# A fused convolution, attention and wavelet block on one core: another order of the first image's stage and of the last tail, with buffers of the tail in the probabilities' place

## The chip, the cores and the metric

The kernel runs on one core of one Trainium2 chip. The metric is the device time of one execution in microseconds (us). The program names the engines so: PE is TensorE (matrix products), DVE is VectorE, ACT is ScalarE, POOL is GpSimd, SP is SyncE, which here only issues DMAs.

## What is computed

The input x has 8 images of 256 channels and 32x32 positions, all float32. Three steps, with L = 1024 positions as tokens:

```python
# 1: attention over positions, 8 heads of 32 channels, on group-normed channels
qkv = einsum('oc,bcl->bol', w_qkv, group_norm(x)) + b_qkv
weight = softmax(einsum('bct,bcs->bts', q * scale, k * scale), axis=1)
x = x + w_proj @ einsum('bts,bcs->bct', weight, v) + b_proj
# 2: linear attention on layer-normed tokens t, with rotated queries and keys
q, k = elu(ln(t) @ Wqk + bqk) + 1
z = 1 / (q . mean(k) + 1e-6);  kv = rope(k)^T v / n
t = t + rope(q) kv * z + lepe(v)          # v = ln(t); lepe: 3-tap depthwise conv
# 3: feed-forward on the low band of a Haar transform of ln(t)
t = t + ffn(ln(t))                        # pair sums, interpolation, fc1, gelu, fc2, back
```

## The kernel before

**The stages.** The work of an image is cut in two. The first half is the softmax attention: 64 units, one for each pair of a key block (8), a head (4) and a head group (2). The second half, "post", is everything behind it: projection, layer norm, linear attention, feed-forward. The program is software-pipelined over images in *bodies*: body i runs the 64 units of image i, the post work of image i-1, and prepares queries, keys and values of image i+1. A prologue comes before body 0, the epilogue ("tail") holds the post work of image 7. So body 0 ("first") has no post work, bodies 1 to 6 are "steady", body 7 is "last".

**A unit.** PE makes the scores of one head and key block into one of two PSUM buffers (`scores`, L653, 128x1024), DVE takes the negated maximum (`maximum`, L1053), ACT takes the exponential with its sum (L914) into `probs`. PE's scores of unit s+1 wait for the exponential of unit s-1, whose buffer they take. After four units DVE inverts the sums (`invert_sums`, L1059), POOL scales the values (`scale_values`, L1330), and PE weighs them (`weigh_values`, L668).

**The order.** Each engine has one queue in which everything else is put between units. Tables of numbers (`PE_FIRST`, `DVE_FIRST`, `PE_TAIL` and so on) give for each piece of work the unit behind which it stands in its engine's queue; `due` reads them. In the tail, where there are no units, the numbers (0 to 63) are only an order. Inside one number the order is that of the table's keys. SP's queue is given by `SP_ORDER`.

**Names.** `pq`, `pk`, `pv` with group 0 or 1: tiles of the next queries, keys, values (L680, L692), each split by ACT (L955) and DVE (L1098) into two parts that SP stacks. `w1`: a weight folded once, in the first body (PE L840, DVE copy L1262). `stats`, `moments`, `gn`, `squares`, `affine`, `apply`: group norm of the next image. `load`: its load. `warm`: two matmuls on constants, whose result nobody reads (`keep_warm`, L867); in the tail they wait only for the last attention copy. In the tail: `proj` (L727), `x1T` (L707), `lnT` (L715), `qk` (L741, eight tiles: group, query or key, half), `kT` (L749, keys to tokens), `kv` (L757), `den`, `denT`, `out` (L781), `uT` (L707), `ll` (L795), `fc1` (L800), `fc2` (L805), `rT` (L715), `rows` (L812).

**Buffers of the tail.** `elu` (L1236) writes queries into `q_ch` (two groups) and keys into `k_ch`, which has room for one group: keys of group 1 wait for the `kT` that reads those of group 0. DVE turns keys (L1181, L1183) into `rot_tok`, with room for one group: turns of group 1 wait for `kv` of group 0. `turn_q` (L507 to L514) multiplies a half-exchanged copy `q_half` of the queries by sines, the queries in place by cosines (after `den` has read them), and adds the two. In the tail POOL turns group 0, and DVE the cosine product and sum of group 1 (`late_turn`). `lepe` taps of channels 0 to 127 are DVE's in the tail (`lepe_tail`, L1250), the others POOL's (L1386, L1389). `probs` holds 2 x 4 x 1024 columns and is not used in the tail.

```python
elif n in (2, 4):
    eng.wait_ge(q_turned[g], 2 * HG * DMA * (b + 1))
    eng.wait_ge(made["den"], b + 1)
    eng.tensor_tensor(q_ch[:, g, :], q_ch[:, g, :], const("cos_ch"), ALU.mult).then_inc(turn_step[g], 1)
```

## Time and profile before

| | |
|---|---|
| median of 3 runs (lowest, highest) | 1364.28 us (1364.17, 1369.44) |
| the profiled execution | 1364.11 us |
| its span, first to last instruction | 1362.3 us |
| mean granted TensorE clock | 0.976 |
| busy share of the span | PE 91%, DVE 73%, ACT 65%, POOL 34% |
| first maximum, first body to second, last maximum | 28.84, 168.00, 1264.60 us |

The first maximum of a body marks its begin here. A busy share is an average over stages; the rows further down are read by stage. "Clock" is the share of 2.4 GHz that TensorE was granted in a stretch: it has two levels, 1.00 (2.4 GHz) and 0.50 (1.2 GHz), and a value between is a mean of the two.

### The profile page before, as it was taken

The numbers are of one execution on the slowest core, as the hardware profiler recorded it, in microseconds if no ns is written. First come the engines' busy times: TensorE is split into PE (matmuls) and PEld (weight loads), VectorE is DVE, ScalarE is ACT, GpSimd is POOL, SyncE is SP. The second block draws the span as 40 slices with busy tenths as digits, with TensorE's granted clock in tenths as the row PEclk, the third lists the DMA queues.
The fourth block names the chain that finished last, engine by engine and source line by source line (L and its number), as shares of the span: only waits on it lengthen the run. The fifth ranks groups of instructions, "written<-read, shape, count | busy, mean of one in ns | idle before, by whom it ended". The sixth has DMA issues, their size and how long they took to land.

```text
span 1362.3 us, 22187 instructions
## 1 busy us (share of the span) xinstructions
PE 1235.3 (91%) x7972; PEld 644.5 (47%) x7972; DVE 995.1 (73%) x1609; ACT 879.5 (65%) x1457; POOL 467.4 (34%) x621
## 2 busy tenths in 40 slices
PE   6888899899998999899998999989998999979796
PEld 5544444544445454445444444454544444444373
DVE  3666687857889487866888578884879678884663
ACT  1666667675776668676775767766685767757422
POOL 2001017520285015630185203840166301850351
PEclk9998999999999999999999999999999999999897
DMA  8242415123442236223351234422262234300210
GB/s 275 58 108 45 106 40 134 34 63 101 110 112 47 52 109 139 48 63 93 92 116 27 66 117 101 105 57 58 88 140 48 62 93 110 80 15 0 80 33 31
DMA packets 51180, 110.84 MB, mean 81 GB/s; under 512 B 15456, under 2 KB 15840, under 8 KB 50816
## 3 DMA queue, kind: packets, MB, share of 16 engines
q1 hardware_dynamic: 48400, 100.39, 30.3%
q0 software_dynamic: 2480, 8.78, 2.3%
q8 instruction: 64, 1.05, 0.3%
q14 instruction: 44, 0.36, 0.1%
q10 hardware_dynamic: 192, 0.26, 0.1%
HBM read 21.81 MB, written 8.39 MB: 22 GB/s over the span
## 4 chain that ended last, share of the span: by engine, by line
PE 54%; DVE 29%; ACT 7%; issue 4%; POOL 2%; DMA 2%; SPq 1%; DVEq 0%; ACTq 0%; POOLq 0%
DVE negmax L1053 15%; PE ps_s L653 13%; PE ps_o L668 7%; PE work L741 6%; ACT probs L914 5%; PE work L680 4%; PE work L800 4%; PE work L727 4%; PE work L692 3%; DVE tok L1129 3%; DVE ln_st L1118 3%; PE work L805 3%; PE work L781 2%; DVE lo L1098 1%; PE work L715 1%
## 5 line engine op out<-in xcount | busy, mean ns | idle before, releaser
L914 ACT ACTIVATE probs<-ps_s,negmax 128x1024 f32<-128x1024 f32 x512 | 571.0, 1115 | 328.0 <-DVE negmax L1053 323.3
L1053 DVE TENSOR_REDUCE negmax<-ps_s 128x1 f32<-128x1024 f32 x512 | 618.8, 1216 | 220.0 <-PE ps_s L653 218.2
L653 PE MATMUL ps_s<-q_st,k_st 128*128 128x512 f32 x1024 | 407.8, 482 | 54.7 <-ACT probs L914 42.7
L653 PEld LDWEIGHTS ps_s<-q_st,k_st 128*128 128x128 f32 x1024 | 165.1, 192 | 294.4 <-ACT probs L914 163.3
L1330 POOL TENSOR_TENSOR v_scaled<-v_tok,rsums 128x128 f32<-128x128 f32 x128 | 56.0, 438 | 580.3 <-DVE rsums L1059 580.3
L668 PE MATMUL ps_o<-probs,v_scaled 128*32 128x512 f32 x2048 | 249.9, 606 | 1.3 <-POOL v_scaled L1330 1.3
L680 PE MATMUL work<-xg,w_qkv 128*128 128x512 f32 x256 | 120.7, 597 | 2.7 <-ACT xg L927 2.7
L741 PE MATMUL work<-ln_ch,w_qk 128*128 128x512 f32 x240 | 115.0, 601 | 3.6 <-DVE k_ch L1236 3.6
L668 PEld LDWEIGHTS ps_o<-probs,v_scaled 128*32 128x32 f32 x2048 | 53.9, 110 | 129.9 <-issue 117.7
L1389 POOL TENSOR_TENSOR x<-x,csum 128x1024 f32<-128x1024 f32 x45 | 107.5, 2389 | 2.5
L914 ACT ACTIVATION_READ_ACCUMULATOR probs<-ps_s,negmax 128x1 f32 x512 | 99.6, 195 | 0.0
L1361 POOL TENSOR_TENSOR ln_var<-ln_mv,con 128x2 f32<-128x2 f32 x64 | 12.9, 202 | 184.4 <-DVE ln_mv L1123 184.4
L800 PE MATMUL work<-band,w 128*128 128x512 f32 x120 | 63.6, 666 | 7.8 <-ACT band L996 6.0
L680 PEld LDWEIGHTS work<-xg,w_qkv 128*128 128x128 f32 x256 | 46.6, 189 | 44.2 <-issue 38.3
L692 PEld LDWEIGHTS work<-w_qkv,xg 128*128 128x128 f32 x512 | 63.6, 196 | 4.1 <-DVE lo L1098 1.4
L692 PE MATMUL work<-w_qkv,xg 128*128 128x128 f32 x512 | 64.0, 280 | 0.0
L741 PEld LDWEIGHTS work<-ln_ch,w_qk 128*128 128x128 f32 x240 | 43.0, 188 | 42.7 <-issue 29.8
L727 PE MATMUL work<-att,w_proj 128*128 128x512 f32 x120 | 56.8, 597 | 0.0
L1386 POOL TENSOR_SCALAR csum<-ln_ch,par 128x1024 f32<-128x1024 f32 x45 | 54.9, 1221 | 0.0
L805 PE MATMUL work<-shared,w 128*128 128x512 f32 x112 | 52.6, 592 | 0.0
L999 ACT ACTIVATE shared<-work,par 128x512 f32<-128x512 f32 x60 | 41.0, 689 | 16.2 <-PE work L800 16.1
L988 ACT ACTIVATE t<-work,par_elu 128x512 f32<-128x512 f32 x60 | 41.2, 687 | 10.9 <-PE work L741 10.9
(157 smaller groups left out, 1448.5 us busy)
## 6 DMA issues: line engine op xcount, KB each, us to landing
q_st<-hi SPq DMA_DIRECT2D x128, 128.0 KB, 2.4
q_st<-lo SPq DMA_DIRECT2D x120, 128.0 KB, 2.4
k_st<-t SPq DMA_DIRECT2D x224, 64.0 KB, 2.0
k_st<-hi SPq DMA_DIRECT2D x128, 64.0 KB, 2.8
k_st<-lo SPq DMA_DIRECT2D x128, 64.0 KB, 3.2
x<-in_x SPq DMA_DIRECT2D x8, 1024.0 KB, 6.1
out_x<-ln_ch SPq DMA_DIRECT2D x16, 512.0 KB, 2.8
xg<-in_x POOLq DMA_DIRECT2D x7, 1024.0 KB, 8.6
```

The costliest lines, as they stand in the source:

```text
L653: mm = pe.matmul(ps_s[s % 2][:, half * HALF:half * HALF + HALF], k_st[:, h, j * P:j * P + P], q_st[g][:, h, half * HALF:half * HALF + HALF ...
L668: mm = pe.matmul(ps_o[D * h:D * h + D, cols], v_scaled[:, j % 2, D * h:D * h + D], probs[:, j % 2, h, cols], start=(j == 0), stop=(j == NB ...
L680: mm = pe.matmul(bank(tile)[:, :], w_qkv[:, c, col:col + P], xg[:, c, half * HALF:half * HALF + HALF], start=(c == 0), stop=(c == NC - 1))
L692: mm = pe.matmul(bank(tile)[:, P * n:P * n + P], xg[:, c, P * nb:P * nb + P], w_qkv[:, c, col:col + P], start=(c == 0), stop=(c == NC - 1))
L727: mm = pe.matmul(ps[:, :], w_proj[:, g, P * c:P * c + P], att[:, g, half * HALF:half * HALF + HALF], start=(g == 0), stop=(g == 1))
L741: mm = pe.matmul(ps[:, :], w_qk[:, c, col:col + P], ln_ch[:, c, 1 + half * HALF:1 + half * HALF + HALF], start=(c == 0), stop=(c == NC - 1))
L800: pe.matmul(ps[:, :], w1[:, P * n:P * n + P], band[:, :], start=True, stop=True)\
L805: mm = pe.matmul(ps[:, :], w2[:, k, :], hid[:, k, :], start=(k == 0), stop=(k == 7))
L914: act.activation(probs[:, j % 2, h, :], ps_s[s % 2][:, :], ACT.Exp, bias=negmax[:, s % 4:s % 4 + 1], accum_out=sums[:, j % 2, h:h + 1]).th ...
L1053: dve.tensor_reduce(negmax[:, s % 4:s % 4 + 1], ps_s[s % 2][:, :], AX_X, ALU.max, negate=True)\
L1330: pool.tensor_tensor(v_scaled[:, j % 2, :].rearrange("p (h d) -> p h d", h=HG), v_tok[g][:, j, :].rearrange("p (h d) -> p h d", h=HG), r.t ...
L1389: pool.tensor_tensor(x1[:, c, :], x1[:, c, :], lepe_product, ALU.add).then_inc(lepe_step, 1)
```

## The change

It has three parts.

1. **The first body** has other numbers on PE, ACT, DVE and POOL. The work in it is the same.
2. **The tail** has other numbers on the four engines, and the eight `qk` tiles come in another order: all queries first (both groups), then all keys. It was queries, keys of group 0, then queries, keys of group 1. It has 41 warm pairs instead of 28.
3. **Places in the tail.** Turned queries of both groups, keys of group 1 and turned keys of group 1 are written into `probs` (`q_home`, `k_home`, `turns_home`). With that three waits are left out there: the cosine product's on `den`, group 1's keys' on `kT`, and group 1's turns' on `kv`.

`keep_warm` also leaves out the later `fc2` steps when it looks for the tile whose bank it writes. SP's order is unchanged, and so is the order in bodies 1 to 7.

```diff
 PE_FIRST = {
-    "w1": (25, 28), "pq1": (12, 12), "pv1": (2, 5), "pk1": (19, 22),
...
-    "pq0": (44, 44), "pk0": (47, 52), "pv0": (44, 56),
+    "w1": (25, 27), "pq1": (11, 12), "pv1": (0, 0), "pk1": (19, 20), "gn": (39,), "pq0": (43, 44),
+    "pk0": (49, 56), "pv0": (45, 56), "values": (6, 10, 14, 18, 22, 26, 30, 34, 38, 42, 46, 50, 54, 58, 62),
...
-QK_ORDER_TAIL = [(g, is_k, half) for g in range(NG) for is_k in (0, 1) for half in range(2)]
+QK_ORDER_TAIL = [(g, is_k, half) for is_k in range(2) for g in range(NG) for half in range(2)]
...
+        def q_home(b, g):
+            return q_ch[:, g, :] if b + 1 < B else probs[:, 1, g, :]
+
+        def k_home(b, g, half):
+            return k_ch[:, half, :] if g == 0 or b + 1 < B else probs[:, 1, 2 + half, 0:HALF]
+
+        def turns_home(b, g):
+            if g == 0 or b + 1 < B:
+                return rot_tok
+            return probs[:, 0, 0:2, :].rearrange("p r (b c) -> p r b c", b=NB)
...
             elif n in (2, 4):
                 eng.wait_ge(q_turned[g], 2 * HG * DMA * (b + 1))
-                eng.wait_ge(made["den"], b + 1)
-                eng.tensor_tensor(q_ch[:, g, :], q_ch[:, g, :], const("cos_ch"), ALU.mult).then_inc(turn_step[g], 1)
+                if b + 1 < B:
+                    eng.wait_ge(made["den"], b + 1)
+                eng.tensor_tensor(q_home(b, g), q_ch[:, g, :], const("cos_ch"), ALU.mult).then_inc(turn_step[g], 1)
             else:
                 eng.wait_ge(turn_step[g], 2 * (b + 1))
-                eng.tensor_tensor(q_ch[:, g, :], q_ch[:, g, :], q_half[g], ALU.add).then_inc(qrot_done[g], 1)
+                eng.tensor_tensor(q_home(b, g), q_home(b, g), q_half[g], ALU.add).then_inc(qrot_done[g], 1)
...
                 elif name == "kT":
                     g, half = n // 2, n % 2
-                    if g == 1:
+                    if g == 1 and b + 1 < B:
 
                         dve.wait_ge(made["kv"], 2 * b + 1)
...
                 g, is_k, half = qk_order(b)[m]
-                if is_k and g == 1:
+                if is_k and g == 1 and b + 1 < B:
 
                     dve.wait_ge(made["kT"], 4 * b + half + 1)
```

**PE, first body, units 43 to 47.** L653/L666 are scores, L668/L681 weighed values, L680/L693 two matmuls for each query or key tile, L692/L705 a value tile, L867/L883 warm pairs (the numbers before and after the slash are the lines before and after the change). Before:

```order
L653 MATMUL ps_s<-q_st,k_st 128x512 x4
L680 MATMUL work<-xg,w_qkv 128x512 x4
L692 MATMUL work<-w_qkv,xg 128x128 x8
L653 MATMUL ps_s<-q_st,k_st 128x512 x4
L668 MATMUL ps_o<-probs,v_scaled 32x512 x8
```

After:

```order
L666 MATMUL ps_s<-q_st,k_st 128x512 x2
L693 MATMUL work<-xg,w_qkv 128x512 x2
L666 MATMUL ps_s<-q_st,k_st 128x512 x2
L693 MATMUL work<-xg,w_qkv 128x512 x2
L666 MATMUL ps_s<-q_st,k_st 128x512 x2
L705 MATMUL work<-w_qkv,xg 128x128 x8
L666 MATMUL ps_s<-q_st,k_st 128x512 x2
L681 MATMUL ps_o<-probs,v_scaled 32x512 x8
```

Two query tiles and a value tile stood together between scores; now each has scores ahead of it and behind it.

**PE, tail, from the sixth to the eighth query/key tile.** L741/L754 are two matmuls for each `qk` tile, L749/L762 the keys' transposes, L867/L883 warm matmuls. Before (the sixth tile ends the first row):

```order
L741 MATMUL ps_s<-ln_ch,w_qk 128x512 x8
L741 MATMUL work<-ln_ch,w_qk 128x512 x2
L867 MATMUL ps_o<-con 128x128 x20
L741 MATMUL work<-ln_ch,w_qk 128x512 x2
L749 MATMUL ps_s<-con,k_ch 128x128 x16
```

After:

```order
L754 MATMUL ps_s<-ln_ch,w_qk 128x512 x8
L754 MATMUL work<-ln_ch,w_qk 128x512 x2
L762 MATMUL work<-con,k_ch 128x128 x4
L754 MATMUL ps_s<-ln_ch,w_qk 128x512 x2
L762 MATMUL ps_s<-con,k_ch 128x128 x4
L883 MATMUL ps_o<-con 128x128 x6
L762 MATMUL ps_s<-con,probs 128x128 x4
```

The ten warm pairs ahead of the eighth tile are gone, and a transpose of group 0's keys stands there.

**DVE, tail, from the taps to the key turns.** L1250/L1267 are the taps, L1236/L1253 the elus, L1181/L1198 and L1183/L1200 one turn together. Before:

```order
L1250 SCALAR_TENSOR_TENSOR x<-ln_ch,par,x 128x1024 x3
L1236 SCALAR_TENSOR_TENSOR shared<-work,par_elu,t 128x512 x2
L1236 SCALAR_TENSOR_TENSOR k_ch,ksum<-ps_s,par_elu,t 128x512 x2
L1236 SCALAR_TENSOR_TENSOR shared<-ps_s,par_elu,t 128x512 x2
L1236 SCALAR_TENSOR_TENSOR k_ch,ksum<-work,par_elu,t 128x512 x2
L1181 TENSOR_TENSOR shared<-ps_s,con 128x512
```

After:

```order
L1253 SCALAR_TENSOR_TENSOR shared<-work,par_elu,t 128x512 x2
L1267 SCALAR_TENSOR_TENSOR x<-ln_ch,par,x 128x1024 x2
L1253 SCALAR_TENSOR_TENSOR shared<-ps_s,par_elu,t 128x512 x2
L1253 SCALAR_TENSOR_TENSOR k_ch,ksum<-ps_s,par_elu,t 128x512 x2
L1253 SCALAR_TENSOR_TENSOR probs,ksum<-work,par_elu,t 128x512
L1267 SCALAR_TENSOR_TENSOR x<-ln_ch,par,x 128x1024
L1253 SCALAR_TENSOR_TENSOR probs,ksum<-ps_s,par_elu,t 128x512
L1198 TENSOR_TENSOR shared<-work,con 128x512
```

The taps moved behind the second and the seventh elu, and keys of group 1 go to `probs`.

## Rows read from the trace of the kernel before

**Rows 1.** The page: granted clock by slice, two groups of instructions.
```profile
PEclk9998999999999999999999999999999999999897
...
L1389 POOL TENSOR_TENSOR x<-x,csum 128x1024 f32<-128x1024 f32 x45 | 107.5, 2389 | 2.5
...
L988 ACT ACTIVATE t<-work,par_elu 128x512 f32<-128x512 f32 x60 | 41.2, 687 | 10.9 <-PE work L741 10.9
```

**Rows 2.** Busy time by stretch: first body, two steady ones, the tail.
```profile
core 0: us, PE busy (x) PEld busy (x) DVE busy (x) ACT busy (x) POOL busy (x), PEclk, DMA share, GB/s
28.84:168.00 139.16, 115.12 (x614) 65.31 (x614) 89.41 (x102) 83.94 (x140) 9.06 (x25) 0.94 0.35 84
...
640.29:798.97 158.68, 147.44 (x958) 73.91 (x958) 121.69 (x199) 109.71 (x183) 59.78 (x77) 0.99 0.35 84
...
957.20:1113.01 155.81, 146.16 (x958) 73.41 (x958) 121.89 (x199) 109.56 (x183) 59.75 (x77) 1.00 0.35 85
...
1264.60:1362.30 97.70, 77.61 (x624) 50.24 (x624) 53.66 (x114) 29.24 (x46) 33.68 (x37) 0.90 0.18 50
```

**Rows 3.** Busy time by stretch: pieces of the first body.
```profile
28.84:48.98 20.14, 15.29 (x90) 11.96 (x91) 10.28 (x10) 9.56 (x16) 0.40 (x1) 0.83 0.41 94
48.98:98.34 49.36, 41.82 (x218) 21.11 (x217) 34.24 (x39) 30.52 (x51) 3.18 (x7) 1.00 0.37 89
98.34:114.69 16.35, 12.05 (x74) 6.65 (x72) 11.81 (x17) 9.53 (x18) 1.92 (x8) 1.00 0.24 56
114.69:134.57 19.88, 17.64 (x82) 9.78 (x83) 11.87 (x14) 13.81 (x21) 1.96 (x6) 0.83 0.15 33
134.57:150.97 16.40, 14.23 (x76) 6.97 (x74) 10.31 (x11) 9.26 (x17) 0.80 (x2) 1.00 0.60 153
150.97:168.00 17.03, 14.08 (x80) 8.83 (x80) 10.90 (x14) 11.26 (x19) 0.80 (x2) 0.90 0.30 72
```

**Rows 4.** Order of time, DVE, first body: start, us, instruction, [idle before <-releaser].
```profile
87.22 0.69 DVE L1262 COPY w<-work 128x512 f32<-128x512 f32 x1 [2.63 <-PE work L840]
...
113.48 0.16 DVE L1082 COPY gn_grp<-work 128x4 f32<-128x4 f32 x1 [2.06 <-PE work L698]
```

**Rows 5.** Order of time, PE, first body (a float32 matmul has two records).
```profile
116.13 1.22 PE L653 MATMUL ps_s<-q_st,k_st 128*128 128x512 f32 x2 [2.68 <-ACT probs L914]
...
125.03 3.67 PE L680 MATMUL work<-xg,w_qkv 128*128 128x512 f32 x8 [0.36 <-ACT xg L927]
128.61 2.05 PE L692 MATMUL work<-w_qkv,xg 128*128 128x128 f32 x16
```

**Rows 6.** Order of time, PE, tail.
```profile
1299.53 4.63 PE L867 MATMUL ps_o<-con 128*128 128x128 f32 x40
...
1330.48 1.91 PE L715 MATMUL work<-con,t 128*128 128x128 f32 x8 [2.58 <-DVE t L520]
1335.54 3.65 PE L795 MATMUL ps_s<-con,csum 128*128 128x64 f32 x16 [3.15 <-POOL csum L1395]
```

**Rows 7.** Order of time, DVE and POOL, tail, up to the first normalised product.
```profile
1289.37 5.95 DVE L1250 SCALAR_TENSOR_TENSOR x<-ln_ch,par,x 128x1024 f32<-128x1024 f32 x3 [3.37 <-ACT x L933]
...
1289.72 3.20 POOL L1389 TENSOR_TENSOR x<-x,csum 128x1024 f32<-128x1024 f32 x1
...
1306.35 0.75 DVE L1236 SCALAR_TENSOR_TENSOR k_ch<-work,par_elu,t 128x512 f32<-128x512 f32 x1 [4.47 <-PE ps_s L749]
...
1307.43 0.75 DVE L1236 SCALAR_TENSOR_TENSOR k_ch<-work,par_elu,t 128x512 f32<-128x512 f32 x1 [0.32 <-ACT t L991]
...
1313.28 0.69 DVE L1181 TENSOR_TENSOR shared<-ps_s,con 128x512 f32<-128x512 f32 x1 [2.57 <-PE work L757]
...
1316.01 2.71 DVE L511 TENSOR_TENSOR shared<-shared,con 128x1024 f32<-128x1024 f32 x1
...
1321.19 0.69 DVE L1199 TENSOR_TENSOR t<-ps_s,zden 128x512 f32<-128x512 f32 x1 [0.34 <-PE ps_s L781]
```

**Rows 8.** Order of time, tail: the band's copy on ACT and its last step.
```profile
1339.28 0.59 ACT L996 COPY band<-ps_s 128x512 f32<-128x512 f32 x1 [6.27 <-PE ps_s L795]
...
1354.67 0.75 DVE L1212 SCALAR_TENSOR_TENSOR band<-ps_s,par,band 128x512 f32<-128x512 f32 x1 [16.46 <-PE ps_s L805]
```

More of the change, by code:

```diff
@@ L129 @@
 PE_TAIL = {
[L130 to L134 removed]
+    "rT": (41, 41, 46, 46), "out": (31, 31, 34, 34), "proj": (0, 0, 1, 3), "uT": (29, 32, 35, 39),
@@ L135 @@
+    "x1T": (3, 3, 9, 9), "qk": (13, 13, 15, 15, 15, 16, 16, 17), "kT": (16, 17, 18, 19), "ll": (43,),
+    "warm": (3, 3, 3, 7, 9, 9, 9, 9, 12, 12, 12, 13, 17, 17, 17, 18, 23, 24, 29, 30, 31, 31, 34, 35, 35, 35, 35, 36, 37, 37, 37, 37, 38, 39, 39, 39, 39, 41, 41, 41, 54, 54),
+    "fc1": (46, 46, 46, 46, 46, 47, 47, 53), "den": (21,), "rows": (54, 57), "fc2": (48, 49, 53, 53),
+    "kv": (26, 28), "denT": (24,), "lnT": (9, 9, 12, 12),
 }
 ACT_TAIL = {
-    "x1T": (0, 0, 0, 2), "den": (35,), "bias": (17,), "lnT": (4, 7, 7, 10), "ll": (40,),
@@ L145 @@
 }
 POOL_TAIL = {
-    "pairs": (50, 54, 56, 57), "rsqrt1": (0, 0, 0, 0), "kmean": (21,), "lepe": (2, 3, 4, 7, 13, 31),
-    "rsqrt2": (40, 46, 46, 48), "turn": (11, 34, 34, 39),
+    "rsqrt2": (37, 39, 51, 53), "rsqrt1": (3, 3, 4, 10), "turn": (21, 30, 30, 35), "pairs": (46, 51, 53, 55),
+    "lepe": (13, 16, 17, 18, 19, 23), "kmean": (25,),
 }
@@ L852, in keep_warm @@
                 order = [t for s in range(UNITS) for t in due("PE", kind, s)]
-                later = [t for t in order[order.index(("warm", n)):] if t[0] not in ("values", "warm")]
+                later = [t for t in order[order.index(("warm", n)):]
+                         if t[0] not in ("values", "warm") and t not in LATER_STEPS]
                 tile = later[0] if later else LISTS[i + 2][0]
@@ L1178, in angle @@
                             .rearrange("p (n o d) -> p n o d", n=4, o=1)[:, :, :, a:z].to_broadcast([P, 4, HG, z - a])
-                    straight, turned = (rot_tok[:, r, rows, :].rearrange("p n (h d) -> p n h d", h=HG) for r in range(2))
+                    straight, turned = (turns_home(b, g)[:, r, rows, :].rearrange("p n (h d) -> p n h d", h=HG)
+                                        for r in range(2))
                     dve.tensor_tensor(straight, k_t, angle("cos_tok", 0, D), ALU.mult)
@@ L1235, in elu @@
                 at = 2 * g + half
-                dve.scalar_tensor_tensor(out=k_ch[:, half, :] if is_k else q_ch[:, g, half * HALF:half * HALF + HALF],
+                dve.scalar_tensor_tensor(out=k_home(b, g, half) if is_k else q_ch[:, g, half * HALF:half * HALF + HALF],
                                          in0=bank(("qk", m))[:, :],
```

39 lines of the change are left out of this document (18 added, 21 removed).

## The prediction

> **What bounds the kernel now.** I read the page first, then the busy time by body, then by pieces of the first body, then the order of time on TensorE (PE), VectorE (DVE), ScalarE (ACT) and GpSimd (POOL) in the two places that the change touches. The page gives no single full engine: PE's granted clock is 9 or 8 tenths in nearly every slice, so PE runs at 2.4 GHz with short falls to 1.2 GHz [rows 1]. By body, the first one takes 139.16 us, the other seven 151.6 to 158.7, and the tail after the last maximum 97.70 [rows 2]. In the first body PE is busy 115.12 of 139.16 us, in the fastest steady body 146.16 of 155.81: the steady bodies are full of PE work, the first body and the tail are full of waits. The loop there is a ring: scores on PE, maximum on DVE, exponential on ACT, and back to PE for the next scores in the same bank. Whatever stands in one of the three queues ahead of its next unit stretches the ring.
>
> The program moves nothing in the six steady bodies or the last; SP's order is word for word the same. So the sum has two terms.
>
> **How I worked them out.** I laid the new order beside the old one, engine by engine, kept for each instruction the duration of its row, and started each when the one ahead on its engine was through and what it waits for was done. Laid out in this way, the old first body comes to 138.7 us where the trace has 139.16, and the old tail to within 0.5 us; that is how far I trust the layout.
>
> **Term 1, the first body, piece by piece** [rows 3]. Same instructions, other places.
> - Units 0 to 7: 20.14 now, 20.4 new. Both second-group value tiles now stand behind the scores of unit 1, in the half-clock stretch (0.83 in this piece), and delay unit 2; by unit 3 the two orders are level, since the old one has the first of them one unit later anyway.
> - Units 8 to 31: 49.36 now, 48.1 new. The two query tiles of group 1 run together between scores, as those of group 0 do for 3.67 us [rows 5]; they now stand on either side of a pair of scores. DVE's copy of the folded weights idles 2.63 us for a PE tile issued just before [rows 4], with the next maximum behind it; it now stands two maxima later. That idle time is mostly PE work that stays, so I count 1.3 for both and not their sum.
> - Units 32 to 39: 16.35 now, 14.3 new. Moments and group copy are in one place on DVE; the copy idles 2.06 us [rows 4] while PE's next scores wait 2.68 us [rows 5]. New: the moments one maximum earlier than the copy's pair, so POOL's two small products and PE's means run below the maxima. 2.1 saved.
> - Units 40 to 47: 19.88 now, 17.0 new. Two query tiles (3.67) and a value tile (2.05) stand together between scores, 5.7 us [rows 5]; now they stand behind three different units. Part of the loss is the fall of the clock to 0.83 here, which follows the 2.68 us wait that goes.
> - Units 48 to 55: 16.40 now, 15.1 new. Reciprocals come straight behind the fourth exponential at every step, where the old order had them one unit late, so PE meets its value step ready.
> - Units 56 to 63: 17.03 now, 16.3 new. A key tile and a value tile now share a place, about 3.7 us together, which costs some 0.8; against that the clock is 0.90 in the old piece, and I expect one fall less.
>
> The new pieces sum to 131.2 us against 139.16: **8.0 less**. Bounds: with no half-clock stretch at all the same layout gives 126.8 (12.4 less); with one more such stretch where PE is densest, 134 (5 less). If only the clock-free waits on DVE went (2.63 and 2.06) it would be 4.7 less. I take 8.0 because the waits named are all on the ring.
>
> **Term 2, the tail** (times from the span's start, tail begins at 1264.60).
> - To the first projected tiles nothing changes: residual and band rows land as before. One of the two late rows of the previous image now stands behind the first statistics; the second store goes out some 3 us later, and lands well before its reader, the copies of the normalised channels.
> - *Up to the last key.* PE now has ten warm pairs in 40 matmuls, 4.63 us, ahead of the eighth query/key tile [rows 6], and DVE idles 4.47 us at the seventh because the keys' place must first be read [rows 7]. Both go: one warm pair is left among these tiles, and second keys are put in the probabilities' place. In exchange DVE's three long taps are split two and one among the elus. By the layout the first two taps hold the third and fourth elus until 1298.4 and 1299.0; the keys follow by ACT's pace (a step has a mean of 687 ns [rows 1] and a tile has two, so some 1.3), and the last, behind a tap, starts at 1305.3; it is 1307.43 now [rows 7]: 2.1 gained.
> - *Key turns.* The second pair of turns idles 2.57 us on the first key-value product [rows 7], since it needs its place. That wait goes. Its two turns and a small product took from 1313.28 to 1316.01, so a turn takes some 1.25; four in a row end at 1311.0, where they end at 1315.8 now. 4.8 gained in all.
> - *Turned queries.* DVE's cosine product took 2.71 us [rows 7] with POOL's sum beside it. The new place has the same neighbour, and comes a little earlier in it: 3.05. The wait on the denominators' product goes too, but it was met long before, so it is worth nothing. The first normalised product starts at 1316.4 and not at 1321.19 [rows 7]: still 4.8.
> - *Second norm to the band.* From there to ACT's copy of the band is 18.1 us now (1321.19 to 1339.28), 17.1 new: PE's 16 pair matmuls took 3.65 us at half clock after waits of 2.58 and 3.15 [rows 6]; POOL's pair sums are now spread, and 18 warm pairs stand on PE around this stretch where 6 do now. 1.0 more.
> - *Feed-forward.* 15.4 us from that copy to the band's last step (1354.67) [rows 8]; 14.6 new, since the first tiles do not meet a half clock. 0.8 more. The end is unchanged.
>
> 4.8 + 1.0 + 0.8 = 6.6; I take off 0.4 for a half-clock stretch that I expect at the first norm as now: **6.2 less**. Bounds: 3.1 less if the half clock comes back for ten microseconds in the second norm; 12.7 less if DVE and POOL never held each other up.
>
> The last bound fails by a row: three DVE taps took 5.95 us and POOL's sum beside them 3.20 [rows 7], where 45 such sums have a mean of 2389 ns [rows 1]. They take turns, whole instructions at a time, and my sum keeps that. The Trainium skill says so too (SBUF — State Buffer, "Who interferes with whom": a VectorE instruction with two SBUF inputs and a GpSimd one that reads SBUF hold a shared port against each other for the whole instruction), and that rule speaks against this change, which sets DVE's taps and turned queries beside POOL's sums again. Without it the tail would gain the 12.7.
>
> **Sum.** 8.0 + 6.2 = 14.2 off the profiled execution's 1364.11 us (span 1362.3 plus 1.8 around it) gives 1349.9; its median over the runs, 1364.28, stands 0.2 above it. I say **1350.0 us**, 1.0% faster. About 0.5%, or 6.8 us, is what a measurement of this kernel can tell from no change.
>
> **Rivals.**
> 1. *The clock takes part of it back* (0.13). A further half-clock stretch in the first body (+2.8) and the one in the second norm (+3.1): 1356. For it: the old pieces show such stretches at three places of the first body [rows 3]; the six steady bodies, one program, differ by 2.9 us (155.81 to 158.68), the longer one at a clock of 0.99 and the shorter at 1.00 [rows 2]. Against it: fewer waits over 2 us remain on PE.
> 2. *The first body doesn't follow its waits* (0.06): what is moved is PE work, its sum stays, and another unit is stretched in place of each. Then only the tail gains: 1364.1 - 6.2 = 1357.9, within 0.5%. Against it: PE stands idle 24 us there.
> 3. *The change does not do what it says in the tail* (0.04): the keys' place is free, but DVE finds POOL's sums in the way at each tap and turn, and the tail ends as now. With the first body's gain: 1356.
> 4. *Slower* (0.03): the clock is not given back after the first half-clock stretch, since two value tiles now stand in it and the ring starts later. Pieces with a clock of 0.83 took 20.14 and 19.88 where 16.35 and 16.40 are usual, some 3.6 us a piece; from four pieces on nothing is gained, and with six pieces, 22 us, it is 1372. Against it: the clock came back within the first piece with less work offered.
>
> **Chances.** Forecast 0.74, rivals 0.13, 0.06, 0.04, 0.03. The range takes the forecast's own bounds, 1345.6 (no half clock in the first body) to rival 1 with one microsecond over it: 1345 to 1357. Faster by over 0.5% holds forecast, rivals 1 and 3: 0.91. Within 0.5%: 0.06. Slower: 0.03.
>
> **What would show it.** The first body from first to last maximum about 131 us, no DVE wait over 1.5 us at the copies of weights and group means, and no more than one tile between pairs of scores but at two places. In the tail: no DVE idle time over 1 us between the elus and the last key turn, first normalised product about 51.8 us after the last maximum (56.6 now), the 16 pair matmuls under 3 us. Wrong, if the first body is above 135 or the tail above 95 us; then the clock row of that stretch says whether it was rival 1, and if that is full, the ring has another bound than I think.

## The result and the profile after

Over four runs the changed kernel has a median of **1350.66 us** (1347.21 to 1352.56), the kernel before 1364.91 (1364.17 to 1369.44). The ratio is 0.9885, 95% interval 0.9859 to 0.9911: 1.2% faster, 1350.0 was forecast. The profiled execution took 1351.87 us with a span of 1350.1; before it was 1362.3, so 12.2 us went from the span. The forecast of 14.2 us less fits the medians (14.25 less) better than it fits the stages: the closeness of 1350.66 to 1350.0 is in part luck. The stretch between the two stages has the same program in every kernel here and takes 1091.6 to 1097.2 us in thirteen profiles.

Busy time by stretch of the changed kernel (first body; its six pieces by units 0 to 7, 8 to 31, 32 to 39, 40 to 47, 48 to 55, 56 to 63; the tail), with the columns of [rows 2] and [rows 3]:

```profile
29.19:161.16 131.97, 111.43 (x615) 63.84 (x616) 89.89 (x102) 84.35 (x140) 8.98 (x25) 0.97 0.36 87
1257.65:1350.10 92.45, 80.25 (x680) 53.87 (x680) 54.02 (x113) 28.66 (x46) 33.45 (x37) 0.96 0.19 53
29.19:50.08 20.89, 15.48 (x90) 12.24 (x91) 10.93 (x11) 9.54 (x16) 0.39 (x1) 0.84 0.38 90
50.08:97.67 47.59, 42.02 (x218) 21.56 (x217) 33.95 (x38) 31.18 (x52) 3.17 (x7) 1.00 0.37 92
97.67:112.18 14.51, 11.82 (x74) 6.73 (x72) 11.75 (x17) 10.48 (x19) 1.19 (x4) 1.00 0.27 64
112.18:129.45 17.27, 15.17 (x83) 8.19 (x83) 11.93 (x15) 12.95 (x21) 2.63 (x9) 1.00 0.14 31
129.45:144.55 15.10, 12.51 (x72) 6.50 (x70) 10.37 (x12) 10.19 (x17) 0.80 (x2) 1.00 0.67 175
144.55:161.16 16.61, 14.43 (x85) 8.61 (x86) 10.96 (x13) 10.01 (x17) 0.80 (x2) 1.00 0.29 71
```

The first body lost 7.19 us, the tail 5.25. From the second body's first maximum to the last maximum it is 1096.49 us, where it was 1096.60: nothing moved there. The first maximum comes 0.35 later. 7.19 + 5.25 + 0.11 - 0.35 = 12.2. PE's busy time fell by 3.7 us in the first body with the same instructions: that is matmuls which no longer run at half clock. In the tail it rose by 2.6 with 14 warm pairs more (the table has 42 of them, not 41, and the row counts differ by 56, four records a pair). The counts in PE's rows are records, two for each float32 matmul: a row of x8 is two warm pairs, and a key-value product of 64 matmuls has 128 records, which the prediction and the expectations call matmuls.

The tail of the changed kernel in order of time; first DVE, then GpSimd, PE, ACT and DVE again:

```profile
1283.71 0.75 DVE L1253 SCALAR_TENSOR_TENSOR shared<-work,par_elu,t 128x512 f32<-128x512 f32 x1 [4.35 <-ACT t L1007]
1286.57 4.67 DVE L1267 SCALAR_TENSOR_TENSOR x<-ln_ch,par,x 128x1024 f32<-128x1024 f32 x2 [0.39 <-ACT x L949]
1298.28 0.74 DVE L1253 SCALAR_TENSOR_TENSOR probs<-ps_s,par_elu,t 128x512 f32<-128x512 f32 x1
1303.33 0.74 DVE L1200 TENSOR_TENSOR probs<-ps_s,con 128x256 f32<-128x256 f32 x2
1304.19 3.02 DVE L524 TENSOR_TENSOR probs<-shared,con 128x1024 f32<-128x1024 f32 x1
1307.56 0.29 DVE L1179 TENSOR_TENSOR kv_c<-ps_s,con 128x128 f32<-128x128 f32 x1 [0.34 <-PE ps_s L771]
1311.27 0.69 DVE L1216 TENSOR_TENSOR t<-ps_s,zden 128x512 f32<-128x512 f32 x1 [1.57 <-PE ps_s L796]
...
1294.92 2.36 POOL L1406 TENSOR_TENSOR x<-x,csum 128x1024 f32<-128x1024 f32 x1
1299.17 0.19 POOL L1418 TENSOR_TENSOR ksum_g<-ksum 128x2 f32<-128x2 f32 x1 [1.90 <-DVE probs L1253]
1303.78 2.35 POOL L527 TENSOR_TENSOR probs<-probs,t 128x1024 f32<-128x1024 f32 x1
...
1304.22 0.87 PE L771 MATMUL ps_s<-tok,probs 128*32 128x32 f32 x78 [0.46 <-DVE probs L1200]
1306.64 0.88 PE L771 MATMUL ps_s<-tok,probs 128*32 128x32 f32 x50 [1.55 <-issue]
1308.36 1.91 PE L883 MATMUL ps_o<-con 128*128 128x128 f32 x8
1310.06 1.10 PE L796 MATMUL ps_s<-kv_c,probs 128*128 128x128 f32 x8
...
1327.69 0.59 ACT L1012 COPY band<-ps_s 128x512 f32<-128x512 f32 x1 [3.88 <-PE ps_s L810]
1342.44 0.75 DVE L1229 SCALAR_TENSOR_TENSOR band<-work,par,band 128x512 f32<-128x512 f32 x1 [15.00 <-PE work L820]
```

Counted from the last maximum (1257.65 here, 1264.60 before): last key elu 40.63 (42.83 before), key turns through at 46.4 (51.2), first normalised product 53.62 (56.59), the band's copy on ACT 70.04 (74.68), the band's last step 84.79 (90.07). These milestones measure the experiments too: six steady bodies of about 157 us and single half-clock stretches move a whole run by some 3 us either way. A stage has less of this, but not nothing. The first body takes 131.12 to 132.66 us in six profiles with the changed order and 138.65 to 141.78 in four with the old one; the changed tail takes 90.80, 91.47, 92.45 and 92.54 us in four profiles with the same instructions. A difference of one profile that is smaller than that is not read as an effect below.

### The profile page after: what moved, and what is told of

Its sections match the earlier page's. It is cut to its first block, busy times and chain, and to the rows that moved or that the text cites. A ratio compares the mean times of both kernels' runs of the same rounds, so it can differ in the third digit from the quotient of the medians.

```text
span 1350.1 us, 22293 instructions
## 1 busy us (share of the span) xinstructions
PE 1234.0 (91%) x8028; PEld 646.0 (48%) x8028; DVE 996.0 (74%) x1609; ACT 878.0 (65%) x1457; POOL 466.6 (35%) x621
## 3 DMA queue, kind: packets, MB, share of 16 engines
q8 instruction: 65, 1.06, 0.3%
## 4 chain that ended last, share of the span: by engine, by line
PE 52%; DVE 29%; ACT 8%; issue 5%; POOL 3%; SPq 2%; DMA 1%; DVEq 0%; POOLq 0%; ACTq 0%
DVE negmax L1069 15%; PE ps_s L666 12%; PE ps_o L681 7%; PE work L754 6%; ACT probs L930 5%; PE work L693 5%; PE work L815 4%; PE work L740 4%; PE work L820 3%; PE work L705 3%; DVE tok L1145 3%; DVE ln_st L1134 3%; PE work L796 1%; DVE lo L1114 1%; PE work L728 1%
## 5 line engine op out<-in xcount | busy, mean ns | idle before, releaser
L666 PE MATMUL ps_s<-q_st,k_st 128*128 128x512 f32 x1024 | 407.3, 481 | 51.3 <-ACT probs L930 39.0
L666 PEld LDWEIGHTS ps_s<-q_st,k_st 128*128 128x128 f32 x1024 | 163.8, 191 | 294.0 <-ACT probs L930 161.2
L681 PE MATMUL ps_o<-probs,v_scaled 128*32 128x512 f32 x2048 | 250.0, 606 | 1.3 <-POOL v_scaled L1347 1.3
L693 PE MATMUL work<-xg,w_qkv 128*128 128x512 f32 x256 | 121.0, 597 | 2.9 <-ACT xg L943 2.8
L754 PE MATMUL work<-ln_ch,w_qk 128*128 128x512 f32 x236 | 113.1, 601 | 3.4 <-DVE k_ch L1253 3.4
L681 PEld LDWEIGHTS ps_o<-probs,v_scaled 128*32 128x32 f32 x2048 | 53.8, 110 | 128.6 <-issue 116.6
L693 PEld LDWEIGHTS work<-xg,w_qkv 128*128 128x128 f32 x256 | 46.7, 189 | 43.8 <-issue 37.6
L705 PEld LDWEIGHTS work<-w_qkv,xg 128*128 128x128 f32 x512 | 63.6, 196 | 3.7 <-DVE lo L1114 0.7
L705 PE MATMUL work<-w_qkv,xg 128*128 128x128 f32 x512 | 63.8, 280 | 0.0
L754 PEld LDWEIGHTS work<-ln_ch,w_qk 128*128 128x128 f32 x236 | 42.3, 188 | 42.0 <-issue 29.3
L820 PE MATMUL work<-shared,w 128*128 128x512 f32 x128 | 59.8, 592 | 0.0
L1381 POOL TENSOR_TENSOR ln_rs<-ln_var,con 128x2 f32<-128x2 f32 x64 | 44.7, 699 | 5.0
```

What stands on the lines that cost most here:

```text
L666: mm = pe.matmul(ps_s[s % 2][:, half * HALF:half * HALF + HALF], k_st[:, h, j * P:j * P + P], q_st[g][:, h, half * HALF:half * HALF + HALF ...
L681: mm = pe.matmul(ps_o[D * h:D * h + D, cols], v_scaled[:, j % 2, D * h:D * h + D], probs[:, j % 2, h, cols], start=(j == 0), stop=(j == NB ...
L693: mm = pe.matmul(bank(tile)[:, :], w_qkv[:, c, col:col + P], xg[:, c, half * HALF:half * HALF + HALF], start=(c == 0), stop=(c == NC - 1))
L705: mm = pe.matmul(bank(tile)[:, P * n:P * n + P], xg[:, c, P * nb:P * nb + P], w_qkv[:, c, col:col + P], start=(c == 0), stop=(c == NC - 1))
L754: mm = pe.matmul(ps[:, :], w_qk[:, c, col:col + P], ln_ch[:, c, 1 + half * HALF:1 + half * HALF + HALF], start=(c == 0), stop=(c == NC - 1))
L820: mm = pe.matmul(ps[:, :], w2[:, k, :], hid[:, k, :], start=(k == 0), stop=(k == 7))
```

## The experiments

**The two parts by themselves.** One kernel takes the four `_FIRST` tables alone, the other everything but these.

> The kernel before with the changed tables of the first body alone. Theory (two separate gains): the first body takes 131 to 133 us from its first to its last maximum as in the changed kernel (131.96), the tail stays at 97.0 to 98.5 (97.70), the time is 7 us below the kernel before, ratio 0.995. Rival (the shorter first body is bought with places in the tail, or gives something back later): the tail or a body between moves by over 1 us.

> The changed kernel with the first body's old tables: the tail change alone. Theory: tail 92 to 93.5 us (92.45), first body 138 to 140, time 5 to 6 us below the kernel before, ratio 0.996. Rival (the tail's 5.25 us hang on the clock that the shorter first body leaves): tail above 94.5.

The first took 1355.19 us, ratio 0.9928 (0.9903 to 0.9954), below the 0.995 expected. It has no profile of a fast execution, so what its expectation says of first body and tail stays untested. The second took 1357.65, ratio 0.9948 (0.9924 to 0.9972), with a first body of 141.78 us and a tail of 90.80, both outside what was expected (138 to 140, 92 to 93.5). Together the ratios make 0.9876, and the whole change is at 0.9885. The times fit two separate parts of 0.7% and 0.5%. The tail came out 1.65 us *better* than in the changed kernel, with the same instructions. DVE and GpSimd there:

```profile
1312.65 1.21 DVE L525 TENSOR_TENSOR probs<-shared,con 128x1024 f32<-128x1024 f32 x1
...
1312.75 3.32 POOL L528 TENSOR_TENSOR probs<-probs,t 128x1024 f32<-128x1024 f32 x1
```

GpSimd waited 0.46 us more for a transfer there, so its sum was started 0.10 behind DVE's cosine product and not 0.41 ahead of it. DVE took 1.21 us and GpSimd 3.32; in the changed kernel it is 3.02 and 2.35. So one number of the prediction, 3.05 for that product, was the outcome of a race. It is not where the 1.65 us come from: behind the product DVE waits for the second key-value product either way, 1.83 us here and 0.34 in the changed kernel, and its copy of that starts at 49.57 and 49.91 from the last maximum. The rest is the clock: it is full here, and at half for 3.4 us from 49.1 in the changed kernel.

**The places, taken back and by themselves.** The first kernel is the changed one with `q_home`, `k_home` and `turns_home` returning the old places and the waits back:

```diff
-            return q_ch[:, g, :] if b + 1 < B else probs[:, 1, g, :]
+            return q_ch[:, g, :]
...
-                    if g == 1 and b + 1 < B:
+                    if g == 1:
```

> The changed kernel, its orders untouched, but queries, keys and turns of the tail go back to their old places, with the three waits that belong to them. Theory A, the one of the prediction (the waits on the places carry the gain up to the first normalised product): the key turns of group 1 wait some 2.3 us for the first key-value product, and the tail is 2 to 2.5 us longer than the changed kernel's 92.45. Theory B (GpSimd and the port carry it, the places little): DVE starts its turns 1.8 to 2.3 later, but its cosine product then finds GpSimd's sum nearly through and takes 1.3 to 1.6 where it took 3.0; the tail is 0 to 0.8 longer.

The second is the kernel before with the places and without the waits:

> The kernel before with the places in the probabilities' place and the three waits dropped, all orders as before. Theory A (the places carry it): the 4.47 and 2.57 us of DVE's idle time go and the first normalised product starts 2.5 us or more earlier than 56.6 us after the last maximum; tail 95 or less. Theory B (GpSimd's queue carries it): the turns start 1.5 us earlier, DVE's cosine product then stands beside GpSimd's cosine product and takes 2.5 to 3.1 where it began late before, GpSimd's sums end when they did, and the tail is within 0.7 of 97.70.

Old places in the new order: 1349.98 us, ratio 0.989 (0.9861 to 0.992), a tail of 92.98 against 92.45, a difference inside what the changed tail varies by. DVE's third turn waits 2.25 us for the first key-value product, and then its cosine product takes 1.26, since GpSimd's sum is nearly through:

```profile
1301.27 0.69 DVE L1195 TENSOR_TENSOR shared<-ps_s,con 128x512 f32<-128x512 f32 x1 [2.25 <-PE ps_s L768]
...
1304.00 1.26 DVE L521 TENSOR_TENSOR shared<-shared,con 128x1024 f32<-128x1024 f32 x1
```

New places in the old order: 1362.37, ratio 0.9984 (0.9964 to 1.0004), no difference that can be told. Its tail, 100.19, is outside what either theory named. It is longer than 97.70 in part ahead of the places: in its first norm the clock is 0.66 over ten microseconds (0.83 before), and the first elu starts at 31.95 from the last maximum and not at 30.64. From that elu to the first normalised product it is 25.68 us, and 25.95 before: the places give 0.27. Behind that it loses another 1.45 us, where nothing was changed.

```profile
1303.38 0.75 DVE L1254 SCALAR_TENSOR_TENSOR probs<-work,par_elu,t 128x512 f32<-128x512 f32 x1 [4.87 <-ACT t L1008]
...
1309.30 2.92 DVE L525 TENSOR_TENSOR probs<-shared,con 128x1024 f32<-128x1024 f32 x1
1312.26 3.28 DVE L528 TENSOR_TENSOR probs<-probs,att 128x1024 f32<-128x1024 f32 x1
```

The idle time of 4.47 us at the seventh elu went, and 4.87 us came one elu later: the eighth tile is still behind the ten warm pairs. The 2.57 at the third turn went too, and what it gained DVE lost in the cosine product and the sum, each beside one of GpSimd. Theory B named the cosine product nearly right on both sides, 1.26 and 2.92 us. But that GpSimd's queue carries this stretch is not what the traces show. The chain of work that ended last in the kernel before leaves DVE behind its second turn and stays on PE up to the first output tile:

```profile
1310.05 0.67 DVE shared L1183 x2
1310.72 0.14 issue
1310.86 1.10 PE work L757 x69
1311.96 0.88 issue
1312.84 0.39 PE work L757 x21
1313.23 3.77 PE ps_o L867 x32
1317.00 0.44 PE ps_s L774 x4
1317.43 1.23 PE ps_s L757 x82
1318.66 1.09 PE ps_o L867 x8
```

Eight warm pairs (3.77 us) stand there between the two key-value products. The wait of 2.57 us, the cosine product and GpSimd's sums are all beside this chain: GpSimd's last sum ended at 1317.64, 2.4 us before PE came to the tile that needs it. With the places alone PE still makes its first output tile at 1314.88 to 1315.94, just ahead of DVE's first normalised product at 1316.32, so without the port DVE could have gained 0.4 us at most. With the old places in the new order the second key-value product starts 2.5 us later, but without the stall of 1.55 us described below, and ends 1.1 us later. What the eight warm pairs ahead of the second product cost was not run by itself.

**Places and warm pairs.** The kernel with the places alone, and nine pairs fewer:

```diff
@@ PE_TAIL, the warm pairs up to 16
-    "warm": (14, 15, 16, 16, 16, 16, 16, 16, 16, 16, 16, 16)
+    "warm": (14, 15, 16)
```

> The kernel with the places alone, and nine of the ten warm pairs ahead of the eighth query/key tile gone as well; orders otherwise as before. Theory (a place pays only together with the tile that fills it, and GpSimd's queue has the rest): the eighth tile is made 4 us earlier, the last key elu starts 2.5 to 3 us earlier against the first tap than in the kernel with the places alone (12.7 us behind the first elu there, about 9.5 here), but GpSimd reaches the keys' mean only after its sine product and is some 0.8 to 1 us earlier, so the first normalised product gains 1 to 2.5 us against that kernel's 25.7 us behind the first elu. Rival (the places and the pairs are worth their waits, 4.5 and 2.6 us): it gains 4 us or more.

1363.57 us, ratio 0.9971 (0.9948 to 0.9995). The last key elu starts 9.44 us behind the first (12.74 with the places alone, 12.19 before), the first normalised product 24.04 behind it (25.68, 25.95): 1.64 gained, within what the theory gave. The two edits that the prediction priced at 4.47 and 2.57 us of idle time are worth 1.9 together without the rest of the new order. DVE then waits 2.68 us for PE's output tile at the first normalised product. PE had waited 1.33 us for GpSimd's keys' mean, and then made the eight warm pairs, partly interrupted, in 4.2 us (1311.46 to 1315.63). So GpSimd's queue holds PE up to the keys' mean here, and the warm pairs do behind it. In this kernel, as before, GpSimd's last tap sum stands behind the keys' mean:

```profile
1308.58 0.19 POOL L1419 TENSOR_TENSOR ksum_g<-ksum 128x2 f32<-128x2 f32 x1
1308.86 0.35 POOL L1422 TENSOR_TENSOR kmean<-con,ksum_g 128x4 f32<-128x4 f32 x2
1309.16 2.40 POOL L1407 TENSOR_TENSOR x<-x,csum 128x1024 f32<-128x1024 f32 x1
```

In the changed kernel that sum runs at 1294.92, in time in which GpSimd waited for the last key elu. It takes 2.4 us out of the way of the turned queries; GpSimd's turned queries were not what PE waited for in the kernel before.

**The first body's pieces.** The changed kernel, with moments, group copy and the group norm's copy and apply where they were before, and both query tiles and the value tile together again:

```diff
@@ PE_FIRST
-    "pq0": (43, 44), "pk0": (49, 56), "pv0": (45, 56)
+    "pq0": (44, 44), "pk0": (49, 56), "pv0": (44, 56)
@@ DVE_FIRST
-    "stats": (28, 33, 34, 37), "moments": (38,), "gn": (40,)
+    "stats": (31, 32, 37, 38), "moments": (38,), "gn": (38,)
@@ ACT_FIRST
-    "copy": (35, 36), "apply": (41, 42)
+    "copy": (36, 37), "apply": (40, 43)
```

> The changed kernel, but in the first body the moments, group copy and group-norm copy and apply stand where they did before, and so do the next query tiles (both behind one unit, with the first value tile). Theory (each wait is paid on the ring where it stands, as the prediction has it): units 32 to 39 take 16.2 to 16.5 us where they took 14.51, units 40 to 47 18.4 to 20.0 where they took 17.27, the other pieces are unchanged. Rival (the order elsewhere carries it): these pieces move by less than half of that, or others move too.

```profile
97.26:113.67 16.41, 11.64 (x74) 6.66 (x72) 11.79 (x17) 9.28 (x16) 1.18 (x4) 1.00 0.24 56
113.67:135.20 21.53, 18.04 (x82) 9.88 (x83) 11.87 (x15) 13.79 (x21) 2.63 (x9) 0.84 0.14 31
```

Units 32 to 39 took 16.41 (14.51), units 40 to 47 21.53 (17.27) with the clock at 0.84, and every other piece behind unit 8 stayed within 0.02. The first is as the theory has it. The second is above its range (18.4 to 20.0) and above the 19.88 of the kernel before, so the pieces don't simply add. The clock is no sure companion of the tiles that stand together: with the old first body units 40 to 47 took 19.88 us at a clock of 0.83, 19.36 and 19.26 at 0.91 (`places_alone`, `places_and_warm`) and 18.89 at 1.00 (`tail_alone`). Against 17.27 the order is worth about 1.6 us there and the clock up to 1.0.

**The value tiles in the half-clock stretch.**

```diff
@@ PE_FIRST
-    "pv1": (0, 0)
+    "pv1": (5, 8)
@@ DVE_FIRST
-    "pv1": (1, 3)
+    "pv1": (6, 10)
```

> The changed kernel; in the first body the two second-group value tiles stand behind the scores of units 6 and 9 and not both behind those of unit 1. Theory A (in the half-clock stretch they cost twice, and the ring stands still for it): units 0 to 7 take 17.5 to 19.5 us where they took 20.89, units 8 to 15 15.1 to 16.1 where they took 15.09, the first body is 1 to 2.5 us shorter. Theory B (with less work on PE the clock stays low for longer, or the ring pays for the tiles wherever they stand): the first 16 units take 36 us as before.

1344.69 us, ratio 0.9847 (0.981 to 0.9885). Units 0 to 7 took 18.04 us (20.89), units 8 to 15 15.09 (15.09), the first body 129.09. In the changed kernel the two tiles hold PE for 5.42 us in the half-clock stretch, with the scores of unit 2 behind them; behind units 6 and 9 they run at full clock and the ring has room for them. By the stage this gains 2.87 us over the changed kernel, and units 0 to 7 take 20.05 to 21.59 us in the seven profiles with both tiles behind unit 1, 18.04 and 17.91 in the two with them moved. The half clock itself lasted longer here, to 8.7 us behind the first maximum and not to 7.8, and the stage is shorter all the same.

**The second norm's warm pairs.** The changed kernel without 13 of them.

> The changed kernel without 13 of the warm pairs that stand in the second norm of the tail (20 of the 24 matmul rows behind the output tiles, and those ahead of the last transposes). The kernel before had 10.2 us of half clock there, the changed one none. Theory A (the warm pairs keep the clock): a half-clock stretch of 3 to 10 us comes back 55 to 75 us after the last maximum, and from the first normalised product to the band's last step it takes 1 to 3 us more than 31.17 (53.62 to 84.79). Theory B (the shorter waits of the new order keep it): no half clock there, and 31.0 to 31.4 us.

```profile
1306.81:1339.40 32.59, 28.14 (x127) 19.36 (x127) 14.99 (x40) 9.49 (x14) 6.56 (x12) 0.90 0.00 1
```

From first normalised product to the band's last step it took 32.59 us where the changed kernel took 31.17 at a clock of 1.00; before it was 33.48 at 0.85. Theory A: of the 2.31 us gained here, 1.42 are these warm pairs'. This stretch repeats well: 31.15 to 31.17 us at a clock of 1.00 in eight profiles with all the warm pairs. The run took 1351.11 us, which can't be told from 1350.66.

**GpSimd's neighbour.** Two kernels ask why DVE's cosine product takes 3.02 us. One moves GpSimd's cosine product ahead of the keys' mean (`"turn": (21, 30, 30, 35)` becomes `(21, 30, 24, 35)`), one makes GpSimd's last sum for one column only, so it leaves out the rest of that sum and is read for its time alone (one run, 1350.22 us).

> The changed kernel; in the tail GpSimd's cosine product of group 0's queries stands ahead of the keys' mean and of group 1's sine product, in 2 us where GpSimd waited. Theory A (GpSimd and DVE take turns at the port for whole instructions): GpSimd's last sum starts 1.3 to 2 us earlier, DVE's cosine product meets its end at most and takes 1.2 to 1.6 us (3.02 in the changed kernel), the first normalised product starts at 52.3 or earlier; tail 90.5 to 91.5. Theory B (the 3.02 us are no matter of the neighbour): the product still takes 2.5 to 3.1.

> The changed kernel, where in the tail GpSimd's last sum of the turned queries of group 0 is made for one column of 1024 alone; the other columns keep the product without the sum. Theory A (the port): DVE's cosine product takes 1.2 to 1.3 us and ends 1.8 us earlier, DVE then waits for the second key-value product instead, and the first normalised product starts 0.3 to 1.4 us earlier than 53.62. Theory B: it takes 2.5 us or more with no neighbour too.

It took 1.22 us in the one and 1.21 in the other, so the 3.02 us are the neighbour's doing. That does not make it a gain: with the sum cut short DVE waited 1.55 us for the second key-value product (0.34 in the changed kernel). The tail is 90.61 there, within 0.2 us of the changed order's best, and the clock did not fall at 49 us. With the product moved the tail is 93.56 (90.5 to 91.5 was expected), in a run of 1349.85 (median 1347.06, ratio 0.9867, 0.9835 to 0.99). The keys' mean came late, PE waited 1.15 us for it at the denominators, the first key-value product with it, and the second followed at once and stalled for 2.29 us. The expectation named a gain and had not asked who waits for what is moved behind.

**PE's stall.** In the rows above PE stops for 1.55 us behind record 78 of 128 in the second key-value product and waits for nothing that its row shows.

```diff
@@ PE_TAIL, of the warm pairs those of 23 and 24
-    "warm": (23, 24), "kv": (26, 28), "denT": (24,)
+    "warm": (27, 27), "kv": (22, 28), "denT": (27,)
```

> The changed kernel; on PE, in the tail, the first key-value product stands ahead of four warm matmuls and the denominators' transposes and not behind them, so that the two key-value products of 128 matmuls each no longer run within one after the other. The stall: in two profiles PE stops for 1.5 us behind matmul 78 of the second product, with nothing that it waits for. Theory A (instructions are brought in slower than these short matmuls use them up): with 1.5 us more between the products the stall shrinks to under 0.7 us, the clock does not fall at 49 us after the last maximum, and the first normalised product starts within 52.3. Theory B (the stall belongs to something else, such as the results' bank or the probabilities' place): it stays at 1.5 us before the same matmul, and the tail as it is.

```profile
1295.91 0.97 PE L771 MATMUL work<-tok,shared 128*32 128x32 f32 x91 [0.69 <-DVE shared L1200]
1297.03 0.53 PE L771 MATMUL work<-tok,shared 128*32 128x32 f32 x37 [0.15 <-issue]
...
1299.02 0.88 PE L771 MATMUL ps_s<-tok,probs 128*32 128x32 f32 x78
1300.92 0.64 PE L771 MATMUL ps_s<-tok,probs 128*32 128x32 f32 x50 [1.02 <-issue]
```

1346.33 us, ratio 0.986 (0.9831 to 0.9889), tail 91.24. The clock did not fall at 49 us, and the first normalised product starts at 52.43 (52.3 was asked), though the cosine product took 3.04 again. That is no gain that can be told: with the unchanged order of this stretch and a full clock it starts at 51.80 to 52.83 in four profiles. The stall shrank to 1.02 us, where the theory asked for under 0.7, and a short one came in the first product. It follows neither bank nor place, since both products have it now and the first is in another bank.

**All that helped.** Value tiles later, GpSimd's product early, the key-value products apart, DVE's sum of turned queries ahead of its second copy (`"late_turn": (23, 23)`), and no warm matmul between the second key-value product and the first output tile.

> The changed kernel with four edits that the earlier runs point to: value tiles behind the scores of units 6 and 9; GpSimd's cosine product ahead of the keys' mean; the first key-value product ahead of warm matmuls and denominators' transposes, with the warm matmuls between the second one and the first output tile moved behind the output tiles; DVE's sum of the turned queries ahead of its copy of the second key-value product. Theory: first body 128.5 to 129.5 us (131.96), DVE's cosine product under 1.6 us, the stall in the second key-value product about 1 us and off the path, first normalised product 50.3 to 51.5 us after the last maximum (53.62), tail 88.5 to 90.5 (92.45); the time 4 to 6 us below the changed kernel's 1350.66, so 0.985 of the kernel before. Rival (PE waits longer with the warm matmuls gone, and the clock falls in the second norm instead): a half-clock stretch between 50 and 75 us after the last maximum, tail 91 or more.

**1343.24 us** over six runs (1342.14 to 1347.21), ratio 0.9847 (0.9811 to 0.9884); first body 128.99, tail 90.34, first normalised product 51.03, second norm to the band's last step 31.64 at a clock of 1.00.

```profile
1250.76:1341.10 90.34, 79.33 (x680) 52.68 (x680) 53.38 (x113) 28.46 (x46) 34.42 (x37) 0.97 0.19 54
28.56:157.55 128.99, 110.12 (x615) 62.78 (x616) 90.06 (x102) 84.50 (x140) 8.98 (x25) 0.98 0.37 90
```

By the stages it is 5.1 us shorter than the changed kernel (131.97 + 92.45 against 128.99 + 90.34), by the medians 7.4, where 4 to 6 was expected. The interval of its ratio still overlaps the changed kernel's, by 0.0025, and the value tiles alone had the same ratio, 0.9847. So the first body is the surer of the two stages: 129.09 with the value tiles alone, 128.99 here. The 2.1 us in the tail rest on one profile, and the changed order had 90.80 itself. DVE's cosine product took 2.26 us and not under 1.6, and the stall was 0.35 us.

## Why the prediction was right, and where it was not

**Term 1** said 8.0 less, 7.2 came. By piece, said and measured: 20.4 and 20.89, 48.1 and 47.59, 14.3 and 14.51, 17.0 and 17.27, 15.1 and 15.10, 16.3 and 16.61. The last three have a clock of 1.00, as forecast. Two of the old pieces owe part of their length to a clock that isn't always low with the old order: units 40 to 47 as said above, and units 56 to 63 take 17.03 and 16.99 us at 0.90 but 16.40 and 16.42 at 1.00, so the new 16.61 is no gain against those. In the first piece the orders were to be level "by unit 3". Unit 2 starts 6.14 us behind unit 1, and unit 3 starts 11.75 us behind the first maximum where it was 10.52 before, so they are not level there. Over the whole piece they are: 20.14 to 22.18 us in four profiles of the old order, 20.05 to 21.59 in seven of the new. The gain that was left in it is the value tiles', 2.87. By the means of four and six profiles the first body is 139.68 and 131.95 us, 7.7 less: the term was right in size.

**Term 2** said 6.2 less, 5.25 came.

- *Up to the last key* and *key turns*: 40.7 and 46.5 us forecast from the last maximum, 40.63 and 46.4 measured.
- *Turned queries*: 3.05 forecast, 3.02 measured. It could have been 1.21. Neither number decides the tail, since DVE next waits for the second key-value product.
- *First normalised product*: "still 4.8" was forecast, 2.97 came, at 53.62 and not 51.8. This step failed: it let DVE's queue alone set that start, and it is PE's that does. The second key-value product stalled for 1.55 us, DVE waited 0.34 us for it, the clock fell, and two warm pairs (8 records) that take 1.06 us at full clock stood for 1.91 ahead of the output tile. The trace of before had such a stall to see, 0.88 us in the first product and on the chain shown above. About the clock alone the term would have been nearer: with the same order and a full clock the product starts at 52.01, 52.66 and 52.83 in three profiles.
- *Second norm to the band*: 1.0 forecast, 1.67 came (18.09 to 16.42 us), since no half clock was left there at all. 1.42 for second norm and feed-forward together are the warm pairs'.
- *Feed-forward*: 0.8 forecast, 0.64 came (15.39 to 14.75). The end is unchanged.

The 0.4 taken off for a half clock in the first norm was not needed: that stretch was free of it, and one of 3.4 us came at 49 us instead. All in all the tail's term was 1 us too large in this profile (91.5 was forecast, 90.80 to 92.54 came in four).

**What was right for the wrong reason.** The laid-out order gave the right milestones, but the words named as carriers the two waits of DVE, 4.47 and 2.57 us. Taken alone these are worth 0.27, and their return costs 0.5, less than the tail varies by. The chain of before names other carriers: ten warm pairs (4.46 us) ahead of the eighth tile, which the prediction had, and eight (3.77 us) ahead of the second key-value product, which it did not name. The new order takes both away, and puts the four key turns and a longer stall on the chain in their place. The share of each was not run one by one; of the ten, nine were taken out, on top of the places, for 1.6 us.

**The port.** DVE's cosine product took 1.21 to 1.26 us in the four kernels where GpSimd's sum was cut short, started behind it or was nearly through, 2.92 to 3.31 in those where it starts while one of GpSimd's long products has just begun, and 1.92 to 2.26 in four where the one beside it was half through. In the kernel before it was 2.71, started 0.74 us into GpSimd's sum. With one and the same order it hangs on when the half-exchanged queries land, 0.46 and 1.3 us later in some profiles than in others. The Trainium skill has this rule (SBUF — State Buffer, "Who interferes with whom": a VectorE instruction with two SBUF inputs and a GpSimd one that reads SBUF contend for a shared port, and whoever issues first has it for the whole instruction). The traces agree, down to the race: who is ready 0.1 us earlier runs at full speed, and the other waits for its end.

**Rivals.** The first (the clock takes part back) happened in small, one stretch of 3.4 us at the key-value product. The second fell: the pieces moved about as laid out, the first one aside, which was level. The third fell with the last key elu. The fourth fell: the clock came back at 37.0 us, where it was 36.8 before. Of the signs that the prediction named, the first normalised product about 51.8 us after the last maximum did not come; the 16 pair matmuls took 2.8 us, waits included, and no wait of DVE in the tail between the elus and the last key turn was over 1 us.

## What to carry to other kernels

Take each wait away by itself before it is given a price, and read the chain that ended last: of 7 us of DVE's idle time a third of a microsecond was to be had, because the chain ran through PE's queue, over warm matmuls, and DVE's own ended 0.3 us ahead of it. When two instructions on DVE and GpSimd with SBUF inputs become ready within half a microsecond, give the one on the path its place by order. Work that nobody waits for yet, such as the value tiles, belongs where the clock is full, and warm matmuls behind what is waited for, not ahead of it. Profile the same order more than once before a difference of 1 or 2 us in a stage is called an effect.

## What was not expected of the hardware

PE stopped in the second key-value product at the same record, 78 of 128, in every profile where the two products follow within 0.5 us: for 1.55 us in the changed kernel, and 1.47, 1.19, 1.78, 1.77 and 1.74 in others with the same order. When the second followed at once it was 2.29 us; with about 1.5 us between, 1.02 and 0.35. Where the second product waited 2.80 us for DVE it ran through without a stall:

```profile
1299.93 1.30 PE L768 MATMUL ps_s<-tok,shared 128*32 128x32 f32 x128
1304.03 1.93 PE L768 MATMUL ps_s<-tok,shared 128*32 128x32 f32 x128 [2.80 <-DVE shared L1197]
```

The profile of the DMA queues over 1299 to 1309 us of the changed kernel has no transfer of data, only the queues that bring instructions:

```profile
q8 instruction: 3, 0.05, 1.8%
q14 instruction: 1, 0.01, 0.3%
```

The times of single packets say more. With every stall goes a packet of 16 KB that lands in queue 8, up to 1.4 us before PE stops or up to 0.8 behind that. PE goes on a nearly constant time behind the packet, however long it had stood (us from the span's start):

| kernel | PE stops | packet landed | PE goes on | from packet | stall |
|---|---|---|---|---|---|
| before (first product) | 1311.96 | 1311.42 | 1312.84 | 1.42 | 0.88 |
| after | 1305.09 | 1305.24 | 1306.64 | 1.40 | 1.55 |
| tail_alone | 1313.55 | 1313.61 | 1315.01 | 1.40 | 1.47 |
| values_later | 1300.08 | 1300.48 | 1301.86 | 1.38 | 1.78 |
| turn_early | 1302.32 | 1303.11 | 1304.61 | 1.50 | 2.29 |
| kv_apart | 1299.90 | 1299.54 | 1300.92 | 1.38 | 1.02 |
| together | 1298.57 | 1297.58 | 1298.92 | 1.34 | 0.35 |

Over all twelve stalls of 0.15 us and more in these products, in eleven kernels, it is 1.34 to 1.55 us. With the old places the packet landed at 1302.57, and the second product, started 1.46 us behind that, had no stall. A product of 64 short matmuls (128 records) takes 1.30 us, so PE goes through its instructions faster here than in any other row shown. That PE waits for the next instructions to be brought in thus fits every profile in time as well as in place. It is still read from traces that were made for other questions: the same stall with fewer instructions of the same length was not tried. The row that has "issue" beside it, behind very short matmuls, is what to look for.

After the 1.55 us stall the clock was 0.51 for 3.42 us, after one of 1.78 us in another kernel it did not fall: from one profile to the next the same order can have such a stretch or not.
